# A four-block transformer-like kernel on one core: last stage with keys first, router logits from statistics, 32-column selection, and matmuls of zeros in TensorE's waits

## The reference, cut to what matters

```python
# after the last attention: x is (4, 256, 256)
block_repr = x.reshape(4, 8, 32, 256).sum(axis=2)
keys = einsum('bnh,kh->bnk', block_repr, Wk)
keys = keys / sqrt(mean(keys * keys) + 1e-6) * rms_weight
attn = softmax(einsum('bnh,h->bn', keys, cond[1]))
proj = einsum('bh,kh->bk', einsum('bn,bnh->bh', attn, block_repr), Wo)
y = x + proj                                   # one row for a sequence
ln = (y - mean(y)) / sqrt(var(y) + 1e-6) * ln_gamma + ln_beta
logits = ln @ Wr + br                          # one number for a token
weights, idx = top_k(logits, 32)               # of 256 tokens of a sequence
fx = ln[idx in ascending order]
out_l = gelu(fx @ W1 + b1) @ W2 + b2           # 256 -> 1024 -> 256
out = x + ln; out[idx] += softmax(weights) * out_l
```

## Time and profile before

| | us |
|---|---|
| median of 3 runs | 1064.6 (1063.01 to 1066.11) |
| the profiled execution, its own time | 1065.38 |
| its span, first to last instruction | 1063.6 |
| phase 6, from the first matmul (994.5) to the end of the span | 69.1 |

### The profile page before, as it was taken

How to read it: one execution, slowest core, us unless ns; L and a number is a source line. 1 busy time by engine, 2 the same in 40 slices (tenths; PEclk the granted TensorE clock), 3 DMA queues, 4 the chain that set the end, 5 groups by cost and what they waited for, 6 DMA issues and landing times.

```text
span 1063.6 us, 39442 instructions
## 1 busy us (share of the span) xinstructions
PE 798.4 (75%) x16553; PEld 518.0 (49%) x16647; DVE 613.4 (58%) x2111; ACT 469.3 (44%) x1892; POOL 409.5 (38%) x491
## 2 busy tenths in 40 slices
PE   3778877889889695968769596785656578998617
PEld 3444543335544464645546464564544445665506
DVE  5645454665624676666767666675666643344474
ACT  2423333355642365655546465554544524343201
POOL 0475560264234376581937649193001002220000
PEclk9999999856999899998989899897998999999868
DMA  9000000400000000000000000000031000000001
GB/s 261 9 1 1 2 1 1 148 2 1 2 21 1 13 4 14 4 14 4 10 8 4 13 4 14 4 8 10 4 75 50 4 2 1 2 1 2 1 0 40
DMA packets 32528, 20.15 MB, mean 19 GB/s; under 512 B 23136, under 2 KB 29280, under 8 KB 32352
## 3 DMA queue, kind: packets, MB, share of 16 engines
q1 hardware_dynamic: 27168, 17.04, 5.9%
q10 hardware_dynamic: 5184, 0.59, 0.4%
HBM read 14.47 MB, written 1.05 MB: 15 GB/s over the span
## 4 chain that ended last, share of the span: by engine, by line
PE 56%; DVE 23%; ACT 8%; issue 7%; DMA 1%; SPq 1%; POOL 0%; ACTq 0%; DVEq 0%; POOLq 0%
PE banks L1229 16%; PE banks L1176 5%; DVE work L1514 4%; DVE h_ring L1528 3%; PE banks L1199 3%; DVE gate_r L1510 3%; ACT nzh L1358 3%; DVE pre_n L1519 3%; PE banks L309 2%; PE banks L402 2%; PE banks L374 2%; PE banks L826 2%; PE banks L330 2%; PE banks L1558 2%; PE banks L1640 1%
## 5 line engine op out<-in xcount | busy, mean ns | idle before, releaser
L1229 PE MATMUL banks<-w_qkv,h_ring 128*4 128x64 f32 x12288 | 237.8, 229 | 142.2 <-DVE h_ring L1528 127.0
L1229 PEld LDWEIGHTS banks<-w_qkv,h_ring 128*4 128x4 f32 x12288 | 186.4, 91 | 219.1 <-DVE h_ring L1528 199.4
L1349 ACT ACTIVATE banks<-gate_r 128x8 f32<-128x8 f32 x256 | 46.2, 181 | 185.5 <-DVE gate_r L1510 185.5
L1510 DVE STREAM_TRANSPOSE gate_r<-banks 128x64 f32<-128x64 f32 x256 | 63.9, 250 | 81.5 <-PE banks L1229 77.7
L1514 DVE STREAM_TRANSPOSE work<-banks 128x64 f32<-128x64 f32 x256 | 76.5, 299 | 7.4 <-PE banks L1229 7.2
L1528 DVE TENSOR_TENSOR_SCAN h_ring<-banks,nzh 128x24 f32<-128x24 f32 x256 | 52.8, 206 | 34.9 <-ACT nzh L1358 3.6
L309 PE MATMUL banks<-zero 128*128 128x512 bf16 x218 | 67.0, 403 | 1.0 <-issue 0.6
L1383 POOL TENSOR_TENSOR work<-work 128x512 f32<-128x512 f32 x14 | 17.8, 1268 | 126.7 <-ACT work L1286 126.7
L1521 DVE STREAM_TRANSPOSE banks<-gate_z 128x64 f32<-128x64 f32 x256 | 60.8, 238 | 9.7 <-ACT gate_z L1354 7.1
L1354 ACT ACTIVATE gate_z<-banks 128x64 f32<-128x64 f32 x256 | 57.1, 223 | 21.0 <-PE banks L1229 20.7
L1519 DVE TENSOR_TENSOR_SCAN pre_n<-banks,work 128x16 f32<-128x16 f32 x256 | 48.7, 190 | 27.0 <-DVE work L1514 0.9
(11 more groups left out here) (413 smaller groups left out, 1646.0 us busy)
## 6 DMA issues: line engine op xcount, KB each, us to landing
big<-in_x SPq DMA_DIRECT2D x1, 1024.0 KB, 5.7
w_gate<-in_L_ffn_w_gate SPq DMA_DIRECT2D x1, 1024.0 KB, 5.0
shared<-in_L_ffn_w_down SPq DMA_DIRECT2D x1, 1024.0 KB, 7.6
...
```

Source lines behind the costliest of these rows:

```text
L1229: mm = nc.tensor.matmul(bank[32 * j:32 * j + B, 0:64], h_col(t, c), w_hh[:, c, g, :].rearrange("p (m n) -> p m n", m=KC)[:, :, 32 * j:32 * ...
L1510: nc.vector.transpose(gate_r[:, :], bank_r[:, 0:64]).then_inc(g_tr, 1)
```

## The change

In phase 5 it adds, before the first group, the eight transposes of Wk and Wo with two ACT copies (the zeros there go from ten to six), and a DVE function `router_sums` behind group 2: ones, kq, gamma times Wr by feature, and the sums of gamma times Wr and beta times Wr. In phase 6 the keys are the first matmuls; the square comes from an ACT activation; the copies of x3 move from DVE to ACT, and POOL adds beta to them. ACT makes only one of the two feature halves of y, DVE the other. The logits come from statistics: with a dot product d of y and gamma Wr, taken by 16 matmuls of one moving column (new step dot), logit = rs8 (d - mean sum(gamma Wr)) + constant. The normalised rows are made by ACT, without gamma and beta, off to the side; gamma and beta are applied to the gathered rows `fxT` by feature, and DVE multiplies and adds the 2048-column rows for the output late. The selection of a tile has the 32 columns of its sequence in place of 128. The scatter is 8 matmuls of 32 rows each, in four row groups, in place of 8 of 128 rows. Before the matmul of a wait PE gets zeros: 6, 4, 2, 2, 12, 24 and 4 of them. Three small loads are added on SP.

```diff
+        wkT, woT = (h_ring[:, 512 * n:512 * (n + 1)].rearrange("p (c n) -> p c n", c=KC) for n in range(2))
+        g_of, b_of, r_of, gr_of = (router[:, n, :] for n in range(4))
...
-            keep_warm(10, bank[0])
+            pe.wait_ge(ld_f, 16 * LD_F)
+            for n, w in enumerate((wk, wo)):
+                for hc in range(KC):
+                    for kc in range(KC):
+                        mm = nc.tensor.transpose(bank[n][:, hc * D + kc * P:hc * D + (kc + 1) * P], w[:, kc, hc * P:(hc + 1) * P], ident)
+                mm.then_inc(f_pe, 1)
+            keep_warm(6, bank[2])
...
+            for n, w in enumerate((wkT, woT)):
+                act.wait_ge(f_pe, from_pe("wt", n + 1))
+                nc.scalar.copy(w[:, :, :], bank[n].rearrange("p (a b) -> p a b", a=KC)).then_inc(f_wtc, 1)
...
+            def router_sums():
+                scratch = big_flat[:, 0:D]
+                v.wait_ge(ld_f, 16 * LD_F)
+                nc.vector.memset(ones[:, :], 1.0)
+                nc.vector.tensor_tensor(kq[0:B * NBLK, :], rmsw[0:B * NBLK, :], qrow[0:B * NBLK, :], ALU.mult)
+                nc.vector.tensor_tensor(gr_of, g_of, r_of, ALU.mult)
+                for n, row in enumerate((gamma, beta)):
+                    chain.done(nc.vector.scalar_tensor_tensor(scratch, row, 1.0, wr, ALU.mult, ALU.mult, accum_out=r_sum[:, n:n + 1]))
+                chain.done(nc.vector.tensor_tensor(r_sum[:, 1:2], r_sum[:, 1:2], brc[:, 0:1], ALU.add))
...
+                if G == 2:
+                    router_sums()
...
             next_round(pe, 18)
...
+            for hc in range(KC):
+                mm = nc.tensor.matmul(pO[0:B * NBLK, 0:D], brT[:, hc, :], wkT[:, hc, :], start=(hc == 0), stop=(hc == KC - 1))
+            mm.then_inc(f_pe, 1)
...
+            keep_warm(6, pM[0])
             pe.wait_ge(f_dve, from_dve("score", 1))
             nc.tensor.matmul(pM[2][0:1, 0:B * NBLK], score[0:B * NBLK, :], ident[0:B * NBLK, 0:B * NBLK], start=True, stop=True).then_inc(f_pe, 1)
+            keep_warm(4, pM[0])
             pe.wait_ge(f_dve, from_dve("att", 1))
             nc.tensor.matmul(pO[:, 0:B * NBLK], ones[0:1, :], att[0:1, :], start=True, stop=True).then_inc(f_pe, 1)
+            keep_warm(2, pM[0])
             pe.wait_ge(f_dve, from_dve("attd", 1))
             for kc in range(KC):
                 for hc in range(KC):
                     mm = nc.tensor.matmul(pM[2][:, 64 + kc * B:64 + (kc + 1) * B], woT[:, hc, kc * P:(kc + 1) * P], attd[:, hc, :],
                                           start=(hc == 0), stop=(hc == KC - 1), skip_group_check=True)
             mm.then_inc(f_pe, 1)
+            keep_warm(2, pM[0])
             for n, t, c, blk in tiles(ycT):
                 if (t, c) == (0, 0):
                     pe.wait_ge(f_yT, n + 1)
-                    pe.wait_ge(f_dve, from_dve("x3c", n + 1))
+                    pe.wait_ge(f_dve, from_dve("yd", n + 1))
+                    pe.wait_ge(f_x3, n + 1)
                 mm = nc.tensor.transpose(banks[n][:, t * D + c * P:t * D + (c + 1) * P], blk, ident)
                 if (t, c) == (1, KC - 1):
                     mm.then_inc(f_pe, 1)
+            for n, t, c, blk in tiles(ycT):
+                mm = nc.tensor.matmul(pM[2][:, 128 + 2 * n + t:129 + 2 * n + t], blk, gr_of[:, c:c + 1], start=(c == 0), stop=(c == KC - 1), skip_group_check=True)
+            mm.then_inc(f_pe, 1)
+            keep_warm(12, pM[0])
             pe.wait_ge(f_dve, from_dve("dg", 1))
             for n in range(2):
                 mm = nc.tensor.matmul(pM[n][:, :], ones[:, :], dg[:, 4 * n:4 * n + 4, :].rearrange("p a b -> p (a b)"), start=True, stop=True)
             mm.then_inc(f_pe, 1)
+            keep_warm(24, pO)
             pe.wait_ge(f_dve, from_dve("sel", 1))
+            of = lambda t: slice(TOPK * (t // ST), TOPK * (t // ST + 1))
             for t in range(NT):
-                mm = nc.tensor.matmul(pO[0:1, 0:P], lg[:, t:t + 1], sel[:, t, :], start=(t == 0), stop=(t == NT - 1))
+                mm = nc.tensor.matmul(pO[0:1, of(t)], lg[:, t:t + 1], sel[:, t, :], start=(t % ST == 0), stop=(t % ST == ST - 1), skip_group_check=True)
             mm.then_inc(f_pe, 1)
+            pe.wait_ge(f_lnn, NT)
             for c in range(KC):
                 for t in range(NT):
-                    mm = nc.tensor.matmul(pM[2][:, c * P:(c + 1) * P], ln[:, t, c * P:(c + 1) * P], sel[:, t, :],
-                                          start=(t == 0), stop=(t == NT - 1), skip_group_check=True)
+                    mm = nc.tensor.matmul(pM[2][:, c * P + of(t).start:c * P + of(t).stop], ln[:, t, c * P:(c + 1) * P], sel[:, t, :],
+                                          start=(t % ST == 0), stop=(t % ST == ST - 1), skip_group_check=True)
             mm.then_inc(f_pe, 1)
             for t in range(NT):
-                mm = nc.tensor.transpose(pS[t // 4][:, (t % 4) * P:(t % 4 + 1) * P], sel[:, t, :], ident)
+                mm = nc.tensor.matmul(pS[0][of(t), (t % ST) * P:(t % ST + 1) * P], sel[:, t, :], ident, start=True, stop=True, skip_group_check=True)
             mm.then_inc(f_pe, 1)
-            pe.wait_ge(f_fxc, 1)
+            pe.wait_ge(f_fxc, KC)
             for m in range(FC):
                 for k in range(KC):
                     mm = nc.tensor.matmul(pT[m // 4][:, (m % 4) * P:(m % 4 + 1) * P], w_1[:, k, m * P:(m + 1) * P], fxT[:, k, :],
...
                     mm.then_inc(f_pe, 1)
             pe.wait_ge(f_dve, from_dve("tw", 1))
             nc.tensor.matmul(pM[1][:, 0:1], tw[0:1, :], ones[0:1, 0:1], start=True, stop=True).then_inc(f_pe, 1)
...
                 mm = nc.tensor.matmul(pM[0][:, 0:D], h1T[:, m, :], w_2[:, m, :], start=(m == 0), stop=(m == FC - 1))
             mm.then_inc(f_pe, 1)
+            keep_warm(4, pO)
+            pe.wait_ge(f_dve, from_dve("selTc", 1))
             pe.wait_ge(f_dve, from_dve("xw", 1))
-            pe.wait_ge(f_dve, from_dve("selTc", 2))
+            for t in range(ST):
+                for b in range(B):
+                    r = slice(TOPK * b, TOPK * (b + 1))
+                    mm = nc.tensor.matmul(banks[b][:, t * D:(t + 1) * D], selT[r, t * P:(t + 1) * P], xw[r, :], start=True, stop=True, skip_group_check=True)
+                    if t == ST - 1:
+                        mm.then_inc(f_pe, 1)
...
             next_round(act, 18)
             act.wait_ge(f_pe, from_pe("keys", 1))
-            nc.scalar.copy(ks[0:B * NBLK, :], pO[0:B * NBLK, 0:D]).then_inc(f_ks, 1)
+            nc.scalar.activation(kscr[0:B * NBLK, :], pO[0:B * NBLK, 0:D], ACT.Square, accum_out=kss[0:B * NBLK, :]).then_inc(f_ks, 1)
+            for n in range(4):
+                act.wait_ge(f_pe, from_pe("x3", n + 1))
+                nc.scalar.copy(x3[:, 2 * n:2 * n + 2, :], (pS[0], pS[1], pT[0], pT[1])[n][:, :].rearrange("p (a b) -> p a b", a=2)).then_inc(f_x3, 1)
             act.wait_ge(f_dve, from_dve("sh", 1))
             nc.scalar.activation(att[0:1, :], att[0:1, :], ACT.Exp).then_inc(f_aexp, 1)
             act.wait_ge(f_dve, from_dve("projc", 1))
             for n in range(4):
+                nc.scalar.activation(ycT[:, 0, n * S:(n + 1) * S], xT[:, 0, n * S:(n + 1) * S], ACT.Identity, bias=projT[:, 0, n:n + 1]).then_inc(f_yT, 1)
+            act.wait_ge(f_dve, from_dve("nm", 1))
+            for t in range(NT):
+                nc.scalar.activation(ln[:, t, :], (pS[0], pS[1], pT[0], pT[1])[t // 2][:, (t % 2) * D:(t % 2 + 1) * D], ACT.Identity,
+                                     bias=nm[:, t:t + 1], scale=rs8[:, t:t + 1]).then_inc(f_lnn, 1)
             act.wait_ge(f_dve, from_dve("wsh", 1))
             nc.scalar.activation(tw[0:1, :], tw[0:1, :], ACT.Exp).then_inc(f_wexp, 1)
+            act.wait_ge(f_pe, from_pe("fx", 1))
+            for c in range(KC):
+                nc.scalar.activation(fxT[:, c, :], pM[2][:, c * P:(c + 1) * P], ACT.Identity, bias=b_of[:, c:c + 1], scale=g_of[:, c:c + 1]).then_inc(f_fxc, 1)
...
+            for n in range(4):
+                pool.wait_ge(f_x3, n + 1)
+                nc.gpsimd.tensor_tensor(x3[:, 2 * n:2 * n + 2, :], x3[:, 2 * n:2 * n + 2, :], beta.unsqueeze(1).broadcast_to([P, 2, D]), ALU.add).then_inc(f_x3b, 1)
...
             v.wait_ge(f_ks, 1)
-            ch.done(nc.vector.scalar_tensor_tensor(kscr[0:R, :], ks[0:R, :], 1.0, ks[0:R, :], ALU.mult, ALU.mult, accum_out=kss[0:R, :]))
             nc.vector.tensor_scalar(kms[0:R, :], kss[0:R, :], 1.0 / D, 1e-6, ALU.mult, ALU.add).then_inc(f_dve, 1)
-            ch.done(nc.vector.scalar_tensor_tensor(kscr[0:R, :], ks[0:R, :], 1.0, kq[0:R, :], ALU.mult, ALU.mult, accum_out=kdot[0:R, :]))
+            ch.done(nc.vector.scalar_tensor_tensor(kscr[0:R, :], pO[0:R, 0:D], 1.0, kq[0:R, :], ALU.mult, ALU.mult, accum_out=kdot[0:R, :]))
...
+            v.wait_ge(f_dve, from_dve("projc", 1))
+            for n in range(4):
```

(31 more changed lines are left out.)

62 lines of the change are left out of this document (15 added, 47 removed).

## The result

The changed kernel takes 1056.2 us (median of 10 runs, 1050.1 to 1057.9), the kernel before 1062.3 on the same chips (10 runs, 1059.1 to 1066.1): a ratio of 0.9941, 95% interval 0.9915 to 0.9968, so 0.6% faster. All ratios here are taken from fast runs alone: a few runs over 1.5% above the fastest of their kernel are left out of them, though not out of the medians. The forecast was 1049.9, a gain of 14.7 us on the 1064.6 known then; the medians show 6.2. The profiled execution has its own time of 1057.9 us and a span of 1056.1.

The account below looks back on a forecast made before the run. DVE alone carries the chain from 1013.41 to 1026.67 us, and PE's clock halves after near-idle stretches. Gains of 19.1 us less 4.4 at fx make 14.7, so 1064.6 becomes 1049.9, range 1044.5 to 1057.

Parts of the forecast that it names:

- start of phase 5: Eight transposes replace four of ten zeros at the start of phase 5: loss 0.2 us.
- to srow: Phase 6 start to srow: keys, sixteen transposes and six zeros take 4.25 us instead of 6.28, gain 2.0.
- y to rs8: From y to the variance: DVE has four additions first; gain 0.4 us at full clock, 0 at half.
- rs8 to lb: Logits from statistics: 2.5 us instead of 13.26, gain 10.8 if dot is not late.
- lb, rank, sel: Logits' broadcast at full clock gains 1.8 us; eight selections of 32 columns gain 0.7; rank counting stays.
- wrow: Sixteen instructions of 32 columns, 0.5 us taken instead of 3.57: gain 3.0.
- fx, selT, fxT, h1: Half clock from fx on loses 4.4 us including selT and the first of h1; selT and fxT lose 0.2.
- sc and the end: Scatter in four row groups takes 1.9 us instead of 3.73; gain 0.4, between 0 and 0.9.
- D: Rival: DVE's small softmax steps are each held by one POOL add, 2 to 3 us, 1052.4 us; chance 0.06.
- B: Rival: dot also at half clock and late, part of twelve zeros uncovered, 6 us lost, 1055.9 us; chance 0.27.
- rule on transposes: Transposes don't count as PE-busy, so y and dot stay at half clock, 1055.9 us; chance below 5 in 100.
- A: Rival: full clock throughout, 1045.1 us; chance 0.17.

Follow-up runs that it names:

- a1: Changed kernel with GpSimd's four adds of x3 and beta moved behind VectorE's step dg: 1050.2 us, ratio 0.9889 to the kernel before.
- c2: a1 with the zeros ahead of the logits' broadcast cut from 12 to 6: phase 6 length 54.6 us against 56.9 of a1.
- c3: a1 without the seven stretches of zeros in phase 6: phase 6 length 58.4 us against 56.9 of a1.
- g1: Changed kernel with GpSimd's four adds waiting for the step sh (subtraction of the maximum): phase 6 length 60.0 us.
- c1: a1 with the zeros ahead of the selection raised from 24 to 38: phase 6 length 54.0 us against 56.9 of a1.
- w2: a1 with zeros 6 to 2 ahead of srow, 12 to 6 ahead of lb, 24 to 38 ahead of the selection, and 128-column fx: 1043.1 us, ratio 0.9822.
- e1: a1 with zeros 6 to 2 ahead of srow, 12 to 6 ahead of lb, 24 to 38 ahead of the selection; fx with 32 columns: length 50.6 us.
- a3: Changed kernel without its seven stretches of zero matmuls in phase 6: 1057.0 us, ratio 0.9941 to the kernel before.

## Why the prediction was right, and where not

The sign and the range (1044.5 to 1057) held, the range by 0.8 us only; the time was 6.3 us above the forecast and the gain less than half of it. By its terms, gain against before, from the two timelines (the forecast's 14.7 is this sum less 0.2 for the start of phase 5):

| term | forecast | measured |
|---|---|---|
| to srow | +2.0 | -1.3 |
| srow to proj | 0 | -0.8 |
| proj to y | +0.4 | +0.5 |
| y to rs8 | +0.4 | -0.1 |
| rs8 to lb | +10.8 | +9.1 |
| lb, rank, sel | +2.5 | +2.2 |
| wrow | +3.0 | +2.6 |
| fx, selT, fxT, h1 | -4.6 | -4.8 |
| ol to sc | 0 | -0.1 |
| sc and the end | +0.4 | +0.3 |
| sum (of the unrounded terms) | 14.9 | 7.7 |

**The step that failed** is "To srow": "the four adds on POOL end about 5 us before the variance comes to POOL". They ended 11 us before it, and that was not the question. I asked what waits in POOL's queue behind the adds and not which DVE step runs beside them, though D named this. D's place was right; its price, 2 to 3 us for several steps each held by one add, was too small: one step was held by all four, 3.3 us on this term, and TensorE's idle time behind it put the clock at half for srow to y, 1.2 us more on the next three terms. a1 shows the sum of it by taking only that away: 4.6 us of length, and by the ratios 1.11% gained instead of 0.59%, 0.52% of 1062 or 5.5 us more.

**By its own signs** the prediction fails at a second place: "wrong if zeros delay a step whose input was there". Lb began 1.49 us after dg had ended, behind zeros. Lb was to come 2.5 us after rs8 and came after 4.2, and the last stage was to take near 54 us and took 61.4. The signs of the logits from statistics (no 2048-column group, lb of 1.88 us) and of fx (0.50, 0.22 us an instruction) were there.

**rs8 to lb** was 1.7 short. Dot was not late by more than 0.2 us: it ended at 1015.36, rs8 at 1015.19, with the clock at 0.95, so the lateness of B did not happen. That B's 1055.9 is the time that came is luck. The rest of the term is the twelve zeros, which were to end under the diagonals at 2.5 us and took 4.28, partly at half clock. c2 shows it: with six, lb starts 0.05 us after dg. The rule on transposes that the prediction put below 5 in 100 would have had dot at half clock, which it was not here. But the reading against it was too firm: L1921's 1.87 us lie in the same stretch of the kernel before as the transposes, and in c3 and g1 the clock was at half through the transposes and dot.

**fx** came as forecast, 0.22 us an instruction at a clock of 0.50. Its loss was 2.9 us where I had 3.4, and h1's 1.7 where I had 1.0 for selT and h1 together. The reason given, the idle 3.3 us ahead of wrow "and then 32-column matmuls", had both halves in it: c1 removed the first and won 2.2 us in fx (against g1's fx 1.0), w2 removed the second against e1 and won 1.0 in fx, 0.4 in selT and 1.7 in h1. A (full clock throughout) was false for the changed kernel; in w2 it was true from wrow on, not behind dot.

**The zeros.** The forecast counted on them in the terms to srow, dot, lb and h1. a3 says that they were worth nothing as placed: they cost 1.2 us ahead of srow (c3) or lay in the held product's shadow, and 1.5 ahead of lb.

**sc and the end, wrow, rank** were right within 0.4 us. sc took 1.15 us, 3.2 times faster than the 3.72 before, where I took 2 times from L1614; the other factor of the prediction was the better guide: the Trainium skill, "TensorE: Matmul & The Clock Gate", section Part 3: Packing small matmuls, gives 3.07 times for four row tiles of 512 columns. This trace agrees at 256. The end gained only 0.3 even so, since the adds and stores behind sc set it. The start of phase 5 is not settled: 0.2 us is far below what the start of phase 6 varies by.
